# Last stage of a convolution-attention-gating kernel: projection weights loaded in eight pieces, PSUM copies on ScalarE, a new split between VectorE and GpSimd

## The reference, cut to what matters

```python
x  = L0_attn_inputs                      # (2, 4096, 4096) float32
xn = layernorm(x)
q,k,v = split(conv3(xn, conv_w) + conv_b)          # 3 x 1024 channels
o  = block-causal attention(q, k, v; blocks of 128, 16 heads of 64)
s  = (o @ wo + bo) @ proj_w + proj_b     # (.., 1024) @ (1024, 4096)
# gate: the 8 largest softmax scores of a 64-way router weight a bias mix
g  = silu(xn * w_sum + w_dense @ expert_bias)      # w_dense: 64 wide
return x + s * g
```

## Time and profile before

| what | value |
|---|---|
| time, median of 2 runs | 1848.43 us (1843.08 to 1853.79) |
| the profiled execution's own time | 1844.95 us |
| its span, slowest core (core 7) | 1843.4 us |
| spans of the 8 cores | 1829.6 to 1843.4 us |
| mean granted TensorE clock of the cores | 0.871 to 0.877 of full speed |
| last stage, core 7 | 1578 to 1843 us of the span |

### The profile page before, as it was taken

The page is one execution under the profiler, slowest core; times in us unless marked ns, Lnnn a source line. Parts: engine busy times, 40 slices in busy tenths (PEclk is TensorE's granted clock), DMA queues, the critical chain, the costliest instruction groups (busy, mean ns, idle before and its releaser), DMA issues.

```text
span 1843.4 us, 17777 instructions; the slowest of 8 cores (1829.6 to 1843.4 us)
## 1 busy us (share of the span) xinstructions
PE 1525.8 (83%) x7424; PEld 724.4 (39%) x7424; DVE 426.9 (23%) x708; ACT 339.3 (18%) x373; POOL 185.5 (10%) x165
## 2 busy tenths in 40 slices
PE   0344699999999999999999999988675676399893
PEld 0344444444444444444444444433343444232221
DVE  2877200000000000000000000000325425168986
ACT  1443000000000000000000000059635434112211
POOL 0000111111111111111111111100000000012212
PEclk9867799999999999999999999999755555598976
DMA  5999566666666566666666666734100005904334
GB/s 143 209 240 191 68 73 80 74 75 80 72 78 79 71 79 75 74 81 71 78 79 72 78 78 72 99 61 71 21 1 1 1 1 73 210 4 182 142 133 182
DMA packets 230709, 163.62 MB, mean 89 GB/s; under 512 B 74579, under 2 KB 222291, under 8 KB 226387
## 3 DMA queue, kind: packets, MB, share of 16 engines
q0 software_dynamic: 155360, 92.97, 40.3%
q1 hardware_dynamic: 75270, 69.50, 13.5%
HBM read 220.69 MB, written 16.78 MB: 129 GB/s over the span
## 4 chain that ended last, share of the span: by engine, by line
PE 69%; DVE 11%; ACT 6%; DMA 5%; SPq 4%; issue 3%; another core or an unknown queue 1%; POOLq 0%; DVEq 0%; ACTq 0%
PE pCv L629 54%; PE pWO L910 6%; PE pPr L964 5%; DMA AL<-x 4%; ACT AL L691 2%; SPq L416 2%; DVE AL L784 2%; PE pQ L713 1%; DVE tRs L776 1%; SPq L421 1%; DVE AL L836 1%; ACT L691 1%; DVE tSc L762 1%; DVE tStat L320 1%
## 5 line engine op out<-in xcount | busy, mean ns | idle before, releaser
L629 PE MATMUL pCv<-AL 128*128 128x512 bf16 x4608 | 1002.9, 380 | 1.0 <-DVE tWmT L550 1.0
L629 PEld LDWEIGHTS pCv<-AL 128*128 128x128 bf16 x4608 | 450.0, 98 | 553.8 <-issue 4.5
L762 DVE TENSOR_REDUCE tSc<-pS 128x1 f32<-128x512 f32 x32 | 21.8, 683 | 1190.0 <-PE pS L755 1190.0
L575 POOL DMA_DIRECT2D AL<-cw x144 | 126.0, 875 | 1056.3 <-PE pCv L629 862.9
L644 ACT ACTIVATE AL<-pCv,tCbT 128x512 bf16<-128x512 f32 x48 | 29.1, 690 | 889.1 <-PE pCv L629 889.1
L964 PE MATMUL pPr<-AL 128*128 128x512 bf16 x512 | 142.0, 427 | 45.8 <-DMA AL<-pw 27.9
L454 PE MATMUL pLgT<-AL 128*64 128x128 bf16 x768 | 61.2, 260 | 128.4 <-DMA AL<-AL 128.4
L910 PE MATMUL pWO<-AL 64*128 64x256 bf16 x512 | 109.8, 414 | 5.7 <-DVE AL L836 5.7
L454 PEld LDWEIGHTS pLgT<-AL 128*64 128x64 bf16 x768 | 60.1, 139 | 129.3 <-issue 129.3
L964 PEld LDWEIGHTS pPr<-AL 128*128 128x128 bf16 x512 | 48.8, 105 | 133.0 <-issue 96.2
L910 PEld LDWEIGHTS pWO<-AL 64*128 64x128 bf16 x512 | 73.2, 144 | 41.4 <-issue 6.6
(11 more groups left out here) (85 smaller groups left out, 740.2 us busy)
## 6 DMA issues: line engine op xcount, KB each, us to landing
AL<-cw POOLq DMA_DIRECT2D x144, 512.0 KB, 5.9
AL<-x SPq DMA_DIRECT2D x16, 2048.0 KB, 12.3
out<-AL SPq DMA_DIRECT2D x8, 2048.0 KB, 7.2
AL<-pw POOLq DMA_DIRECT2D x1, 8192.0 KB, 64.5
AL<-wq POOLq DMA_DIRECT2D x1, 2048.0 KB, 18.2
AL<-wk POOLq DMA_DIRECT2D x1, 2048.0 KB, 14.0
AL<-wv POOLq DMA_DIRECT2D x1, 2048.0 KB, 14.6
AL<-wo POOLq DMA_DIRECT2D x1, 2048.0 KB, 15.0
```

The lines of the kernel that those rows point to most:

```text
L575: sCWs[gi % 4].add(e.dma_start(out=cwr[:, gi % 4, :].rearrange("p (g f) -> p g f", g=8), in_=d_cw[s, g].rearrange("g p f -> p g f")), 16)
L629: ins = e.matmul(p_cv[:, 512 * (bs + 2 * sub + hf): 512 * (bs + 2 * sub + hf) + 512], lhsT, xnTh[:, o:o + 512], start=(step == 0), stop=(s ...
L762: cNM.add(e.reduce_max(nmax[Q % 2][:], p_S[:, 512 * (Q % 2):512 * (Q % 2) + 512], axis=AX.X, negate=True), 1)
```

## The change

- `proj_w` is loaded by eight DMAs, one for each piece kc, and each is issued only when the one before has landed.
- In tile 0 PE goes piece by piece: for each kc it waits for that piece and multiplies it for all 8 segments; the bias matmuls follow at the end. Tiles 1 to 7 keep the old order.
- The 8 copies out of PSUM go from DVE to ACT (with the wait for the store of tile tt-2).
- The product and the addition of x are split at column 1536 in place of 2048 (product) and not at all (addition): POOL takes columns 0 to 1535 of both, DVE the other 2560. POOL's addition for tile tt-1 stands behind its product for tile tt.
- SP waits for both halves of the addition (cFIN and cPLe) before it stores tile tt-1 and loads x for tile tt+1.

```diff
-                sPW.add(e.dma_start(out=pwv,
-                                    in_=d_pw.rearrange("(c p) f -> p c f", p=128)), 16)
+                pwsrc = d_pw.rearrange("(c p) f -> p c f", p=128)
+                for kc in range(8):
+                    if kc >= 1:
+                        e.wait_ge(sPW.h, 16 * kc)
+                    sPW.add(e.dma_start(out=pwv[:, kc, :], in_=pwsrc[:, kc, :]), 16)
...
                     if tt == 0:
...
-                        e.wait_ge(sPW.h, 16)
...
+                        for kc in range(8):
+                            e.wait_ge(sPW.h, 16 * (kc + 1))
+                            for seg in range(8):
+                                e.matmul(p_pr[:, 512 * seg:512 * seg + 512],
+                                         aoT[:, kc, 0:128],
+                                         pwv[:, kc, 512 * seg:512 * seg + 512],
+                                         start=(kc == 0), stop=False)
...
-                @DV
+                @AC
                 def _(e, tt=tt):
-                    ins = e.tensor_tensor(t_sc3[:], t_r[:, tt:tt + 1],
-                                          t_wsum[:, tt:tt + 1], ALU.mult)
-                    cSC3.add(ins, 1)
                     if tt >= 2:
                         e.wait_ge(sSTs[tt % 2].h, 16 * (tt // 2))
                     for seg in range(8):
                         e.wait_ge(cPE6.h, 16 * tt + seg + 1)
-                        cSev.add(e.tensor_copy(s6[tt % 2][:, 512 * seg:512 * seg + 512],
-                                               p_pr[:, 512 * seg:512 * seg + 512]), 1)
+                        cSev.add(e.activation(
+                            s6[tt % 2][:, 512 * seg:512 * seg + 512],
+                            p_pr[:, 512 * seg:512 * seg + 512], AF.Copy), 1)
...
-                    e.wait_ge(cSC3.h, tt + 1)
+                    dedge(e, e.tensor_tensor(t_sc3[:], t_r[:, tt:tt + 1],
+                                             t_wsum[:, tt:tt + 1], ALU.mult))
...
-                        cFIN.add(e.tensor_add(s6[(tt - 1) % 2], s6[(tt - 1) % 2],
-                                              x6[(tt - 1) % 2]), 2)
+                        cFIN.add(e.tensor_add(s6[(tt - 1) % 2][:, 1536:4096],
+                                              s6[(tt - 1) % 2][:, 1536:4096],
+                                              x6[(tt - 1) % 2][:, 1536:4096]), 1)
...
                     e.wait_ge(cSIL.h, tt + 1)
-                    cPL.add(e.tensor_mul(s6[tt % 2][:, 0:2048], s6[tt % 2][:, 0:2048],
-                                         gw[:, 0:2048]), 1)
+                    cPL.add(e.tensor_mul(s6[tt % 2][:, 0:1536], s6[tt % 2][:, 0:1536],
+                                         gw[:, 0:1536]), 1)
+                    if tt >= 1:
+                        cPLe.add(e.tensor_add(s6[(tt - 1) % 2][:, 0:1536],
+                                              s6[(tt - 1) % 2][:, 0:1536],
+                                              x6[(tt - 1) % 2][:, 0:1536]), 1)
...
                     if tt >= 1:
-                        e.wait_ge(cFIN.h, 2 * tt)
+                        e.wait_ge(cFIN.h, tt)
+                        e.wait_ge(cPLe.h, tt)
                         sSTs[(tt - 1) % 2].add(
                             e.dma_start(out=d_out[128 * (tt - 1):128 * tt, :],
                                         in_=s6[(tt - 1) % 2]), 16)
```

More of the change, by code:

```diff
@@ L959, in _ @@
                         e.wait_ge(cOTe.h, 128)
-                    for seg in range(8):
-                        if tt >= 1:
-                            e.wait_ge(cGI.h, 8 * (tt - 1) + seg + 1)
-                        for kc in range(8):
-                            e.matmul(p_pr[:, 512 * seg:512 * seg + 512],
[L965 to L975, removed]
@@ L977, in _ @@
-                @DV
+                        for kc in range(8):
[5 more added lines that the diff above has]
+                                         start=(kc == 0), stop=False)
+                        for seg in range(8):
+                            e.matmul(p_pr[:, 512 * seg:512 * seg + 512],
+                                     t_ones2[0:1, :],
+                                     pbhi[0:1, 512 * seg:512 * seg + 512],
+                                     start=False, stop=False)
+                            cPE6.add(e.matmul(p_pr[:, 512 * seg:512 * seg + 512],
+                                              t_ones2[0:1, :],
+                                              pblo[0:1, 512 * seg:512 * seg + 512],
+                                              start=False, stop=True), 1)
+                    else:
+                        for seg in range(8):
+                            e.wait_ge(cGI.h, 8 * (tt - 1) + seg + 1)
+                            for kc in range(8):
+                                e.matmul(p_pr[:, 512 * seg:512 * seg + 512],
+                                         aoT[:, kc, 128 * tt:128 * tt + 128],
+                                         pwv[:, kc, 512 * seg:512 * seg + 512],
+                                         start=(kc == 0), stop=False)
+                            e.matmul(p_pr[:, 512 * seg:512 * seg + 512],
+                                     t_ones2[0:1, :],
+                                     pbhi[0:1, 512 * seg:512 * seg + 512],
+                                     start=False, stop=False)
+                            cPE6.add(e.matmul(p_pr[:, 512 * seg:512 * seg + 512],
+                                              t_ones2[0:1, :],
+                                              pblo[0:1, 512 * seg:512 * seg + 512],
+                                              start=False, stop=True), 1)
@@ L1034, in _ @@
                     e.wait_ge(cSIL.h, tt + 1)
-                    dedge(e, e.tensor_mul(s6[tt % 2][:, 2048:4096],
-                                          s6[tt % 2][:, 2048:4096],
-                                          gw[:, 2048:4096]))
+                    dedge(e, e.tensor_mul(s6[tt % 2][:, 1536:4096],
+                                          s6[tt % 2][:, 1536:4096],
+                                          gw[:, 1536:4096]))
                     cPL.add(e.engine_nop(), 1)
@@ L1055, in _ @@
                 e.wait_ge(cPL.h, 16)
-                cFIN.add(e.tensor_add(s6[7 % 2], s6[7 % 2], x6[7 % 2]), 2)
+                cFIN.add(e.tensor_add(s6[7 % 2][:, 1536:4096],
+                                      s6[7 % 2][:, 1536:4096],
+                                      x6[7 % 2][:, 1536:4096]), 1)
+            @GP
+            def _(e):
+                e.wait_ge(cPL.h, 16)
+                cPLe.add(e.tensor_add(s6[7 % 2][:, 0:1536], s6[7 % 2][:, 0:1536],
+                                      x6[7 % 2][:, 0:1536]), 1)
             @SY
             def _(e):
-                e.wait_ge(cFIN.h, 16)
+                e.wait_ge(cFIN.h, 8)
+                e.wait_ge(cPLe.h, 8)
                 sSTs[7 % 2].add(e.dma_start(out=d_out[128 * 7:128 * 8, :],
```

## The result

The changed kernel takes 1913.49 us (median of 11 runs, 1900.45 to 1921.21) against 1848.43 us before. The ratio is 1.0344, with a 95% interval of 1.0313 to 1.0375: slower, by some 64 us by the ratio (the two medians lie 65 us apart). The forecast was 1903 us, slower by 2.9%.

What follows compares the result with a forecast made beforehand. It took the load of x, released late behind POOL's addition, to set the period: 1617 + 36 + 221 + 27.3 = 1901.3, put at 1903 us on the profiled execution's own time, 2.9% slower; range 1883 to 1918.

Steps and rivals of the forecast that it cites:

- The step that carries the forecast: Tiles 2 to 7: next load of x waits behind POOL's product and addition, these behind SiLU; 36.8 us a period.
- Rival A: Tiles 2 to 7: copies' relief counts, load of x stays hidden; period 20.5, time 1805, 2.3% faster; 4%.
- T7: Landing of the last of eight proj_w pieces, put at 1617 (1605 to 1635), 12 us later than the one load.
- T7 to the end of tile 1's additions: Tiles 0 and 1: 12.4 us from T7 for tile 0; tile 1's additions end at T7 + 36 = 1653.
- six periods: Tiles 2 to 7: the loop of 36.8 us, PE waiting for x through DVE, gives 221 us.
- tail: After the last gate additions: SiLU, products, additions sharing one port, store; 27.3 us, against 23.0 before.
- The price of a piece: Loads of proj_w: 8.6 us for each 1024 KB piece, 8.8 with 0.2 for POOL to wake.
- the collision with the loads of x: Last two proj_w pieces run beside two loads of x: 6 us lost, half of 12 us of full engines.
- Rival C: Pieces of proj_w slow or losing much to x: T7 = 1635, time 1921; sign, landing after 1628; 10%.
- DVE's additions follow at that pace: Tile 0: additions keep up with ACT's copies, 4.8 us, so tile 0 ends 12.4 us after T7.
- rival B: Product and addition: POOL gets the port first and keeps it for both; 2.9 us less a period, time 1885; 10%.
- DVE's relief buys nothing: Tiles 2 to 7: taking the copies (4.8 us) off DVE gains nothing, since PE waits for x through DVE.

Runs made afterwards that it cites:

- number 1: Changed kernel with POOL's addition for a tile directly behind its product of that same tile: 1841.49 us, ratio 0.9961.
- number 4: Kernel before plus one SP wait: store and load of x issued only after both products of the tile: 1886.24 us, ratio 1.0189.
- number 6: Kernel before with copies on ACT, and a tile's product and addition both on DVE behind its SiLU, POOL doing nothing in the last stage: ratio 0.9752.
- number 11: number 8 with SiLU and product in two halves of 2048 columns, the first behind four gate additions: 1788.50 us, ratio 0.9714.
- number 10: Changed kernel with SP issuing the load of x ahead of the store: 1911.01 us, ratio 1.0378.
- number 2: Changed kernel with POOL's addition struck out, the addition of x wholly on DVE: 1852.34 us, ratio 0.9997.
- number 5: Kernel before with only the copies out of PSUM moved from DVE to ACT: 1828.58 us, ratio 0.9879.
- number 8: number 6 with the kc order and proj_w in eight loads issued at once, a semaphore for each: ratio 0.9726.

## Why the prediction was right

**The loop, and the sign.** The step that carries the forecast, that x is released behind POOL's addition and this behind SiLU, is shown in both directions: undoing the order alone takes the ratio from 1.0344 to 0.9961 (number 1, some 70 us), and a late release alone makes the old kernel 1.89% slower (number 4). Rival A, the hidden load at 1805, did not come: a period near its 20.5 appears only when the release is early (21.75 in number 6, 20.76 in number 11). The prediction gave it a wider gate than its own terms allow: with 0.3, 2.57 and 4.87 us behind the landing, a period of 20.5 needs x within 12.8 us of the last gate addition, not 20, and the steps ahead of the load alone are 15.1.

**The sum, term by term.** On core 0 it is 1920.6 against the 1901.3 forecast, 19.3 more. All four terms were low, so none covers another. The median of the 11 runs lies in the forecast's range of 1883 to 1918, and the profiled execution above it; part of the 19.3 belongs to this one execution.

| term | forecast | measured | difference |
|---|---|---|---|
| last piece lands, T7 | 1617 | 1624.5 | +7.5 |
| T7 to the end of tile 1's additions | 36 | 39.4 | +3.4 |
| six periods | 221 | 229.2 | +8.2 |
| tail | 27.3 | 27.5 | +0.2 |

*T7.* In the chain of core 0 the last two pieces are these:

```profile
1598.45 15.74 DMA AL<-pw
1614.24 0.47 issue
1614.72 9.79 DMA AL<-pw
```

The price of a piece, 8.6 us and 0.2 for POOL to wake, was near for cores 1 to 7: medians of 8.2 to 8.7 us, and then 0.5 until the next one starts. No row had shown the 0.2. On core 0 the median is 9.9. The term that was mis-sized is the collision with the loads of x, set at 6 us, half of their work. On cores 1 to 7 the one piece that fell beside them took 17.2 to 19.5 us, 9 to 11 more than the others. On core 0 the loads of x met the sixth and seventh piece, 11.3 and 15.7 us, and the whole took 86.8 us from the first issue: 16.4 beyond eight times 8.8, of which 9.4 are these two pieces. The first issue, at 1537.7, came 3 us earlier than the 1540.7 of the sum. Rival C stayed out by a little: its sign was a landing after 1628.

*Tile 0 and 1.* From the landing it took 16.2 us and not 12.4. Start of the last eight piece matmuls, table load, gate matmuls and additions on core 0:

```profile
1624.65 3.57 PE L965 MATMUL pPr<-AL 128*128 128x512 bf16 x8 [6.75 <-DMA AL<-pw]
...
1635.09 3.59 PE L1011 MATMUL pPr<-AL,tWmT 64*128 64x512 bf16 x8
```

```profile
1629.27 1.28 ACT L1001 ACT_TABLE_LOAD   x1 [45.27 <-PE pPr L974]
```

```profile
1635.80 4.87 DVE L1030 TENSOR_TENSOR AL<-AL,pPr 128x512 f32<-128x512 f32 x8 [31.80 <-PE pPr L1011]
```

The first segment was complete after 4.8 us, as forecast. The step of this term that failed is "DVE's additions follow at that pace": the gate matmuls stand behind all sixteen bias matmuls in PE's list, and these ran at the granted clock of 0.50 (1.2 GHz), 0.43 us each, so that the additions started only at T7 + 11.3. Tile 1 itself took 23.3 against the 23.6 in the sum.

*The period.* Its engine parts came out as worked out: from the end of SiLU to that of POOL's addition 9.6 us (1782.56 to 1792.15), as forecast, and DVE's product was first in every tile, so rival B did not come. The term that was too small is the load of x, taken at 14.0 (12.6 to 14.8) in the belief that rarer loads meet fewer others. It took 15.2 to 16.2 us on core 0, outside those bounds and above the 14.8 of the earlier trace rows; here is the line view of L1073 (core 0):

```profile
DMA to landing us min/median/max: 15.2/15.5/16.2
```

Why is open. On cores 0, 1, 6 and 7 the median is 15.5 to 16.0 (on core 7 it was 12.6 before), on cores 2 to 5 it is 11.6 to 12.8. Cores 6 and 7 issue theirs within 1.7 us of each other (1712.20 and 1710.95 in tile 2), and 0 and 1 within 3.1, while 2 and 3 lie 4 to 6 us apart and 4 and 5 over 8. That fits neighbours who collide when in step; no run tested it. It isn't always the same cores: in the run of 1915.97 us only cores 6 and 7 have spans above 1900. Over six periods these 3 to 4 us make some 20 of the 34 us by which the spans now differ.

The sum says that ACT's copies end before x has landed, with the store at 6.6 us, its time at the end of the program. They did, but with little to spare, for the store took 9.2 us (median, core 0) beside the load:

```profile
1763.89 1.28 ACT L1001 ACT_TABLE_LOAD   x1 [19.13 <-DMA out<-AL]
1765.19 4.03 ACT L1001 ACTIVATE AL<-pPr 128x512 f32<-128x512 f32 x8
```

The last copy is out at 1769.22, and DVE starts on x at 1770.11. That fits number 10, where exchanging the two issues gained nothing.

*The tail.* DVE's addition of tile 7 and POOL's two additions share the port, as worked out (core 0):

```profile
1904.28 3.41 POOL L1050 TENSOR_TENSOR AL<-AL 128x1536 f32<-128x1536 f32 x1
1907.66 5.99 POOL L1086 TENSOR_TENSOR AL<-AL 128x1536 f32<-128x1536 f32 x1
```

```profile
1904.42 5.95 DVE L1079 TENSOR_TENSOR AL<-AL 128x2560 f32<-128x2560 f32 x1 [3.38 <-POOL AL L1047]
```

DVE's 2560 columns take 5.95 us here and 2.83 where it had the port: it sat out POOL's addition until 1907.7, and POOL's next one then sat out DVE. By the Trainium skill, page "SBUF — State Buffer", section "Who interferes with whom", the one that comes second is blocked for the whole instruction of the first; the trace agrees.

**The parts of the change.** Taken alone the pieces cost 0.65% and the copies on ACT bring 1.21%. Together with POOL's early addition they give 0.39% (number 1), and without any addition on POOL 0.03% (number 2); the intervals of these two overlap, so that POOL's share of the addition shows no clear gain even in the right place. One of the three ideas brought time, one cost a little, and the third lost 3.8% by its place in a list. For "DVE's relief buys nothing" DVE's wait of 20 us a tile for x speaks; no run of the changed kernel takes the copies back. In the kernel before the same relief is worth 22 us (number 5), since in some tiles there the copies did end last.

## What to carry to other kernels

Before moving part of an operation to another engine, follow what its completion releases: with double buffers, an addition that may be done "any time before the store" also frees the buffer of the next load, and its place behind a later tile's wait made a transfer of 12 to 16 us, which had been hidden in some tiles, part of every period. Make the last use of a buffer at the earliest point of its own tile; the kernel that does so with DVE doing more work and POOL none (number 6, proj_w in one load) is 2.5% faster than the one before, where the changed kernel is 3.4% slower. Once the transfer is off the path, price the engine moves again: the copies' move was worth 22 us before and about 44 after.

## What the runs showed of the hardware

- Of eight DMAs of 1024 KB issued in 4.3 us (number 8) the longest took 48.6 to 51.6 us, by core, while one DMA for the same 8192 KB took 53.6 to 67.2 us (number 6). Issued one behind the other they took 8 to 11 us each, and 15.7 to 19.5 us beside two loads of 2048 KB.
- Exchanging the two issues of SP exchanged the landing times of load and store: on core 6 the medians of 16.0 and 9.3 us became 9.5 and 13.8. On every core the one issued first took 7.1 to 10.0 us and the second 11.6 to 16.0 (medians).
- After 6.75 us of waiting for the last piece PE ran 32 matmuls at the low clock, some 14 us, busy all the time from 1624.65 to 1638.7 (granted 0.50). In the earlier trace rows, after 27.9 us of waiting, it was back at 2.4 GHz behind its first segment, 4.3 us: granted 0.50 to 1608 and 1.00 from 1610. The longer idle time was followed by the shorter stretch at the low clock; why, no run shows.
